# Where r is projected, who adds the diagonal term, and the order of work in the two feed-forward fronts of a hybrid block

## The chip, the core and the metric

The kernel runs on one core of a Trainium2 chip, as one launch. The metric is the device time of that launch in microseconds; lower is better. Engines are named as in the profile: PE is TensorE (PEld its weight loads), DVE is VectorE, ACT is ScalarE, POOL is GpSimd, SP issues most DMAs. Each engine runs its own list of instructions in the order in which the kernel writes them, and the lists meet only at semaphores.

## What is computed

Input x has 2 sequences of 1024 tokens with 128 channels, all float32. Every layer is added to x after a layer norm of its input:

```
x = x + attn_a(layernorm(x))   # 16 heads of 8, decaying state, token shift, group of 32
x = x + ffn(layernorm(x))      # shared SwiGLU + one expert of 32 for each token
x = x + attn_b(layernorm(x))   # 16 heads of 64, blocks of 16, 5 levels of coarse keys
x = x + ffn(layernorm(x))      # the same weights again
```

In attn_a, for one token, `y = inter + intra + diag * v`, with `diag = sum(r * (time_faaaa * k))` over a head. The kernel reads inter and intra together out of one recurrence over the tokens; diag * v is the "diagonal term". In ffn, `scores = sigmoid(max logit)`, the tokens are sorted by expert, and `silu(x g) * (x u)` times d is computed for each group.

## The kernel before, in words

The 2048 tokens are worked in 4 chunks of 512 (STEPS = 4).

**Attention A** (`a_pe`, `a_act`, `a_pool`, `a_dve`, about 0 to 120 us). Each engine has a loop over the chunks c. For one chunk PE projects v, k, r (`project`, L275 and L276: two products of 128x512 each) into the banks WIDE[0..2]; ACT copies them out (`projected`, L500). PE spreads the rows of v over four banks (`spread_rows`, L291), twice per chunk; it waits for the copies of all three of v, k and r. DVE multiplies k by the spread v (`key_value`, L751, 8 per chunk in two fours) and runs the recurrence (`scan`, L757, 8 per chunk). POOL multiplies the states by r (`weigh`, L660), PE sums them per head (`pick`, L299, two halves) into the bank YB. The diagonal term: PE sums r*k per head (`diagonal`, L310), ACT copies it, POOL multiplies it by v (`dv`), and PE adds it to the sums in YB by a product with the identity (`add_diagonal`, L305); ACT copies YB out (`copy_y`, L511). PE turns y (`turn_y`, L317), DVE takes its statistics, ACT normalises, PE turns it back (`turn_back`, L323), ACT copies, PE projects (`project_y`, L334), and DVE adds it to x (`add_output`, L763). Beside this the next chunk is prepared: `turn_x`, `mix_in` (L242), ACT's tanh, `mix_out` (L249), and DVE's `mixed` (L734, after scans 0 and 1 of the chunk before).

**Front of a feed-forward layer** (`f_pe`, `f_act`, `f_dve`, `f_pool`, k = 0 and 1). Per chunk: statistics, `front_norm`, `front_turn` (L999), `front_copy`, `front_logits` (L1009), `route` (DVE, L1028 to L1035: best expert and its one-hot). `count_tokens` counts per expert for each half of the tokens, `first_places` / `second_places` and `row_numbers` turn the counts to row numbers; POOL then scatters each half with 8 indirect DMAs (L1475) to sorted_x. The shared expert runs beside it: `shared_half` (L1157), `gate_shared` (ACT, L1173), `product_shared` (DVE, L1179), `shared_out` (L1166), `add_shared` (L1184). Two places hold products whose result nobody reads: L1203 (k = 0) and `keep_clock` (L1194). Then 24 runs of 128 sorted rows follow (L1253 and on), each group of 32 rows with its expert's weights.

**Attention B** (`b_pe` and its companions, about 200 to 450 us). It begins with 4 unread products (L1709), x's first two chunks normalised by DVE (L1464) with POOL's power (L178), turned, copied by ACT and projected (L1738). Then come 16 units of two heads. `project_out` (L1831) of a unit needs POOL's product of output and reciprocal (L2210, two halves), and DVE adds it to x (`gather_out`, L2060). After the last unit the second front begins: `first_slots`, the sums of chunks 2 and 3, and so on.

## Time and profile before

| | us |
|---|---|
| median of the runs shown | 547.14 (545.95 to 549.12) |
| the profiled execution, its own time | 546.38 |
| its span in the trace | 544.6 |
| mean granted TensorE clock | 0.974 of full |

| engine | busy us | share |
|---|---|---|
| PE | 489.6 | 90% |
| PEld | 300.6 | 55% |
| DVE | 424.8 | 78% |
| ACT | 290.7 | 53% |
| POOL | 251.4 | 46% |

Read it by stages: attention A to about 120 us, first front to 150, first runs to 200, attention B to 450, second front to 485, second runs to the end. A timeline row names an instruction (or a row of like ones), its start, its length, and in brackets how long its engine had stood idle before it and whose result ended that. A share of busy time is a mean over stages; what a wait is worth is read from the stage where it stands.

### The profile page before, as it was taken

What the parts mean: (1) busy time and instruction counts of PE and PEld (TensorE: products, weight loads), DVE (VectorE), ACT (ScalarE), POOL (GpSimd) and SP (SyncE); (2) the same over time, 40 slices, a digit from 0 to 9 for tenths busy, and PEclk for the clock granted to TensorE, in tenths of its full rate; (3) what the DMA queues carried; (4) which work ended last, traced back from release to release, by engine and by line L of the source; (5) the groups of instructions that cost most, each with busy time, mean ns of one, the idle gap of its engine ahead of it and who ended that gap; (6) DMA issues with size and microseconds to landing.
All of it is one profiled execution on the core that took longest, in us unless ns stands there. A gap on an engine that the chain in (4) does not pass through costs nothing.

```text
span 544.6 us, 16679 instructions
## 1 busy us (share of the span) xinstructions
PE 489.6 (90%) x6456; PEld 300.6 (55%) x6456; DVE 424.8 (78%) x979; ACT 290.7 (53%) x624; POOL 251.4 (46%) x294
## 2 busy tenths in 40 slices
PE   6899899778999988999989999999999778989991
PEld 3323333344545445677767777677767666444540
DVE  3498899987557767788898888998978987657762
ACT  3743533446288835566455655456544324448870
POOL 3578766746425461533544433333313535524542
PEclk9999999989999989999999999999999987999996
DMA  6799840001588832000000000000000000268964
GB/s 186 305 427 300 83 49 2 0 0 41 165 234 271 269 104 69 17 22 22 22 17 27 23 14 17 14 22 22 22 22 9 6 4 19 57 189 280 279 205 139
DMA packets 45326, 54.11 MB, mean 99 GB/s; under 512 B 10880, under 2 KB 36416, under 8 KB 44224
## 3 DMA queue, kind: packets, MB, share of 16 engines
q1 hardware_dynamic: 42688, 47.78, 30.3%
q0 software_dynamic: 2560, 5.26, 2.8%
q8 instruction: 52, 0.85, 0.7%
q14 instruction: 26, 0.21, 0.1%
HBM read 43.55 MB, written 9.48 MB: 97 GB/s over the span
## 4 chain that ended last, share of the span: by engine, by line
PE 61%; DVE 22%; issue 5%; POOL 4%; DMA 3%; ACT 3%; SPq 0%; POOLq 0%; DVEq 0%; ACTq 0%
PE psum L1253 9%; PE psum L1738 7%; PE psum L1756 7%; PE psum L1831 5%; PE psum L1272 4%; PE psum L1810 4%; PE psum L1260 3%; DVE arena L757 3%; POOL sorted_x L1475 2%; PE psum L1779 2%; PE psum L275 2%; DVE arena L2040 2%; PE psum L1820 2%; DVE arena L2035 2%; DVE arena L2081 2%
## 5 line engine op out<-in xcount | busy, mean ns | idle before, releaser
L2210 POOL TENSOR_TENSOR arena<-arena 128x512 f32<-128x512 f32 x32 | 40.9, 1299 | 108.4 <-issue 102.2
L1503 POOL DMA_INDIRECT y_tok<-arena,to x48 | 46.5, 969 | 64.9 <-ACT arena L1322 63.7
L1926 ACT ACTIVATE arena<-psum 128x512 f32<-128x512 f32 x64 | 37.9, 597 | 45.2 <-PE psum L1738 42.0
L1738 PE MATMUL psum<-arena 128*128 128x512 f32 x128 | 59.2, 605 | 0.8 <-ACT arena L1909 0.7
L1253 PE MATMUL psum<-experts,arena 128*32 x96 | 50.2, 604 | 1.0 <-ACT arena L1312 1.0
L1253 PE MATMUL psum<-arena 128*32 128x512 f32 x288 | 50.9, 605 | 0.0
L1756 PE MATMUL psum<-arena 128*128 128x128 f32 x384 | 47.5, 278 | 1.5 <-ACT arena L1931 1.5
L1756 PEld LDWEIGHTS psum<-arena 128*128 128x128 f32 x384 | 45.2, 191 | 2.5 <-ACT arena L1931 2.5
L2147 POOL TENSOR_TENSOR arena<-arena 128x256 f32<-128x256 f32 (+4 forms) x75 | 33.9, 451 | 24.9 <-ACT arena L1945 18.3
L660 POOL TENSOR_TENSOR arena<-arena 128x512 f32<-128x512 f32 x32 | 37.1, 1180 | 16.4 <-DVE arena L757 12.0
L1738 PEld LDWEIGHTS psum<-arena 128*128 128x128 f32 x128 | 22.9, 189 | 35.6 <-issue 34.0
L1336 ACT ACTIVATE arena<-experts 128x768 f32 x48 | 40.1, 839 | 1.9 <-issue 1.7
L1399 DVE COPY arena<-psum 128x256 f32<-128x256 f32 x48 | 20.4, 425 | 25.0 <-PE psum L1260 25.0
L1475 POOL DMA_INDIRECT sorted_x<-arena,row x32 | 31.1, 973 | 18.6 <-DVE row L1103 10.1
L757 DVE TENSOR_TENSOR_SCAN arena<-psum,arena 128x512 f32<-128x512 f32 x32 | 39.2, 1267 | 0.1
L1810 PE MATMUL psum<-arena 64*64 64x64 f32 (+2 forms) x1728 | 36.8, 224 | 2.4 <-ACT arena L1941 1.5
L1934 ACT ACTIVATE arena<-psum 128x512 f32<-128x512 f32 x48 | 28.7, 598 | 16.4 <-PE psum L1756 16.4
L1272 PEld LDWEIGHTS psum<-experts,arena 128*32 128x32 f32 x192 | 20.7, 110 | 29.8 <-issue 29.6
L2060 DVE TENSOR_TENSOR x_tok<-x_tok,psum 128x512 f32<-128x512 f32 x30 | 20.6, 687 | 20.8 <-PE psum L1831 20.7
L1810 PEld LDWEIGHTS psum<-arena 64*64 64x64 f32 x1728 | 33.0, 137 | 6.5 <-ACT arena L1941 1.6
L1831 PE MATMUL psum<-arena 128*128 128x128 f32 x256 | 34.0, 286 | 2.7 <-POOL arena L2210 2.7
L2034 DVE TENSOR_REDUCE arena<-psum 128x16 f32<-128x1024 f32 (+1 forms) x32 | 30.4, 950 | 3.4 <-PE psum L1779 2.9
(240 smaller groups left out, 1180.6 us busy)
## 6 DMA issues: line engine op xcount, KB each, us to landing
arena<-in_experts SPq DMA_DIRECT2D x48, 384.0 KB, 4.4
experts<-in_experts SPq DMA_DIRECT2D x8, 1536.0 KB, 17.7
arena<-sorted_x SPq DMA_DIRECT2D x48, 64.5 KB, 3.9
sorted_x<-zeros SPq DMA_DIRECT2D x2, 1536.0 KB, 15.3
arena<-in_w_qkv SPq DMA_DIRECT2D x16, 192.0 KB, 3.1
arena<-y_tok SPq DMA_DIRECT2D x8, 256.0 KB, 3.2
x_tok<-in_x SPq DMA_DIRECT2D x4, 256.0 KB, 4.3
arena<-in_w_out SPq DMA_DIRECT2D x16, 64.0 KB, 1.9
```

The costliest lines, as they stand in the source:

```text
L757: dve.tensor_tensor_scan(a_state[:, m, 1:CHUNK + 1], DECAYS[:, :], a_kv[m % HALF], a_state[:, m, 0:1], ALU.mult, ALU.add).then_inc(s["stat ...
L1253: mm = pe.matmul(bank[2 + s % 2][rows, :], f_gxt[s % 2][:, rows], weights, start=True, stop=True)
L1272: mm = pe.matmul(bank[6 + s % 2][SLOT_ROWS * j:SLOT_ROWS * j + SLOT_ROWS, 0:C], f_sht[s % 2][:, rows], weights, start=(half == 0), stop=(h ...
L1336: act.activation(f_w_act[s % 5], experts[:, bass.ds(expert_at[s], WROW)], ACT.Copy).then_inc(t["w_act"], 1)
L1475: pool.indirect_dma_start(out=sorted_x[k], out_offset=bass.IndirectOffsetOnAxis(ap=f_row[:, i:i + 1], axis=0), in_=row_of(k, i), in_offset ...
L1503: pool.indirect_dma_start(out=y_tok, out_offset=bass.IndirectOffsetOnAxis(ap=f_to[:, s:s + 1], axis=0), in_=f_gy[(s + 4) % 8], in_offset=N ...
L1738: pe.matmul(ring("in", n, j)[:, :], b_w[n % 2][:, which * P:which * P + P], x, start=True, stop=True)\
L1756: mm = pe.matmul(ring("in", n, 5 + i // 4)[:, i % 4 * P:i % 4 * P + P], x, b_w[n % 2][:, 2 * P:3 * P], start=True, stop=True)
L1810: mm = pe.matmul(place(Y[r][out]), b_v[n % 2][rows, i, out], e[rows, head, i - part.start, cols], start=(i == 0), stop=last_place(r, i, cols))
L1831: mm = pe.matmul(ring("out", n, i // 4)[:, i % 4 * C:i % 4 * C + C], b_yn[:, i * P:i * P + P], b_wo[n % 2], start=(n < LAST - 1 or n < LAS ...
L1926: act.activation((b_q, b_k)[which][:, part * CHUNK:part * CHUNK + CHUNK], src, ACT.Copy, scale=(D_B ** -0.5, 1.0)[which]).then_inc(h["drai ...
L2210: pool.tensor_tensor(b_yn[:, part], b_y[:, part], b_rec[:, part], ALU.mult).then_inc(h["normed"], 1)
```

## The change

Attention A. `project(c, 2)`, the projection of r, moves from the end of chunk c - 1 to behind `spread_rows(c, 0)`, and goes to the bank OB instead of WIDE[2]; `spread_rows(c, 0)` now waits for the copies of v and k alone, `mix_in(c)` for that of r. `add_diagonal` on PE and `copy_y` on ACT are gone; `outputs(c)` on DVE adds YB and the diagonal term into a_y, behind scan(c + 1, 1), and for the last chunk behind the first route. `turn_back` and `copy_back` of the earlier chunks go to the start of the chunk after next.

First front (k = 0). The two unread products go; the second product of the shared expert's chunk 0 goes behind `route` of chunk 3.

Start of attention B. The add of chunk 1's expert outputs is done in the last runs, both powers are behind each other on POOL ahead of the last two scatters, two unread products instead of four, and q and k are projected chunk by chunk (`project_half`, `drain_half`).

End of attention B and second front (k = 1). Five short unread products (`fill_wait`) stand around the last unit's coarse scores. The second half of the last unit's output is multiplied by DVE (`normalise_late`) and not by POOL. The shared expert's first pair of products goes ahead of the last `project_out`, three unread products behind. `first_slots` goes behind the last sums, `first_places` behind the last chunk's norm, `shared_out` behind `count_tokens`, and `add_shared(0)` behind `slot_experts`, which is the tail of `second_places`, now its own function. `keep_clock` is left out for k = 1.

```diff
                 pe.wait_ge(s["mixers"], 2)
-                after(pe, s["decay_exp"], c)
+                after(pe, s["rkv"], 3 * c)
...
-                if c > 0:
+                if n == 2:
+                    pe.wait_ge(s["decay_exp"], c + 1)
+                elif c > 0:
                     pe.wait_ge(s["kv"], N_A * (c - 1) + HALF + n + 1)
-                pe.matmul(WIDE[n][:, :], weights, a_x[c % 2][:, 1:CHUNK + 1], start=True, stop=False)
-                pe.matmul(WIDE[n][:, :], weights, a_t[(2, 1, 3)[n]], start=False, stop=True).then_inc(s["proj"], 1)
+                pe.matmul(PROJECTED[n][:, :], weights, a_x[c % 2][:, 1:CHUNK + 1], start=True, stop=False)
+                pe.matmul(PROJECTED[n][:, :], weights, a_t[(2, 1, 3)[n]], start=False, stop=True).then_inc(s["proj"], 1)
 
             def spread_rows(c, q):
                 if q == 0:
                     pe.wait_ge(s["rows"], 1)
-                    pe.wait_ge(s["rkv"], 3 * c + 3)
+                    pe.wait_ge(s["rkv"], 3 * c + 2)
                     pe.wait_ge(s["shifted"], 2 * c + 2)
...
-            def add_diagonal(c):
-                pe.wait_ge(s["dv"], c + 1)
-                pe.matmul(YB[:, :], ident, a_diag, start=False, stop=False).then_inc(s["dvacc"], 1)
 
...
             project(0, 0)
             turn_x(1)
-            project(0, 2)
 
...
                 if now:
                     spread_rows(c, 0)
-                if back and now:
-                    add_diagonal(c - 1)
+                    project(c, 2)
+                if 2 <= c < STEPS:
+                    turn_back(c - 2)
...
                     pe.wait_ge(s["kv"], N_A * c + HALF + 1)
                     front_turn(pe, 0, 0)
                     keep_busy_last(1)
                     pe.wait_ge(loaded_later, LATER_LOADS * 16)
                     front_logits(pe, 0, 0)
-                if next_:
-                    project(c + 1, 2)
-                if back:
+                if c >= STEPS - 1:
                     turn_back(c - 1)
...
                     after(act, s["g"], N_A * (c - 1))
-                act.activation((a_v, a_k, a_r)[n][c % 2], WIDE[n][:, :], ACT.Copy).then_inc(s["rkv"], 1)
+                act.activation((a_v, a_k, a_r)[n][c % 2], PROJECTED[n][:, :], ACT.Copy).then_inc(s["rkv"], 1)
 
             def copy_diagonal(c):
                 act.wait_ge(s["diag_in"], c + 1)
-                after(act, s["dvacc"], c)
+                after(act, s["y"], c)
                 act.activation(a_diag, YB[:, :], ACT.Copy).then_inc(s["diag"], 1)
-
-            def copy_y(c):
-                act.wait_ge(s["picked"], 2 * c + 2)
-                act.wait_ge(s["dvacc"], c + 1)
-                after(act, s["yt"], c)
-                act.activation(a_y, YB[:, :], ACT.Copy).then_inc(s["y"], 1)
 
...
+            heads_and_rows()
             projected(0, 0)
-            heads_and_rows()
             copy_x(1)
-            projected(0, 2)
-            norm_x(2)
             for c in range(STEPS + 1):
                 now, next_, later_, back = c < STEPS, c + 1 < STEPS, c + 2 < STEPS, 1 <= c
                 if now:
                     decay(c)
+                    if c == 0:
+                        norm_x(2)
+                    projected(c, 2)
...
 
+            def outputs(c):
+                dve.wait_ge(s["picked"], 2 * c + 2)
+                dve.wait_ge(s["dv"], c + 1)
+                after(dve, s["yt"], c)
+                dve.tensor_tensor(a_y, YB[:, :], a_diag, ALU.add).then_inc(s["y"], 1)
+
...
                 for m in range(HALF):
                     key_value(c, m)
+                scan(c, 0)
+                scan(c, 1)
+                if back:
+                    outputs(c - 1)
                 if c == STEPS - 1:
                     dve.wait_ge(s["rkv"], 3 * STEPS)
                     row_ids(dve, 0)
-                scan(c, 0)
-                scan(c, 1)
...
             add_output(STEPS - 2)
             route(dve, chain, 0, 0, 1)
+            outputs(STEPS - 1)
...
                 front_logits(pe, k, 2)
-                for _ in range(2):
-                    pe.matmul(rows_bank(k, 3)[:, :], ident, shared_up[:, :], start=True, stop=True)
                 front_turn(pe, k, 3)
                 front_logits(pe, k, 3)
                 count_tokens(pe, k, 1)
                 shared_out(pe, k, 0)
+                shared_half(pe, k, 1, 0, 1)
             else:
                 front_turn(pe, k, 2)
+                front_logits(pe, k, 2)
                 front_turn(pe, k, 3)
-                front_logits(pe, k, 2)
                 front_logits(pe, k, 3)
+                shared_half(pe, k, 1, 0, 1)
+                count_tokens(pe, k, 1)
                 shared_out(pe, k, 0)
-                count_tokens(pe, k, 1)
-            shared_half(pe, k, 1, 0, 1)
             shared_half(pe, k, 1, 1, 2)
-            keep_clock(2)
+            if k == 0:
+                keep_clock(2)
             shared_half(pe, k, 2, 0)
...
             else:
                 gate_shared(act, k, 0, 0)
+                gate_shared(act, k, 0, 1)
                 front_norm(act, k, 2)
-                gate_shared(act, k, 0, 1)
                 front_copy(act, k, 2)
                 front_copy(act, k, 3)
...
                 row_ids(dve, k)
-                first_places(dve, chain, k)
-                row_numbers(dve, chain, half_of(k, 0), 0)
             c = STEPS - 1
...
             if k == 1:
+                first_places(dve, chain, k)
+                row_numbers(dve, chain, half_of(k, 0), 0)
+                route(dve, chain, k, 2, 2)
+                product_shared(dve, k, 0, 1)
+                second_places(dve, chain, k)
+                slot_experts(dve, chain, k)
+                add_shared(dve, k, 0)
                 for n in range(2):
-                    product_shared(dve, k, 0, n)
-                route(dve, chain, k, 2, 2)
+                    product_shared(dve, k, 1, n)
             else:
                 route(dve, chain, k, 2, 1)
+                product_shared(dve, k, 0, 0)
+                route(dve, chain, k, 3, 1)
+                product_shared(dve, k, 0, 1)
+                second_places(dve, chain, k)
+                slot_experts(dve, chain, k)
+                add_shared(dve, k, 0)
                 for n in range(2):
-                    product_shared(dve, k, 0, n)
-                route(dve, chain, k, 3, 1)
-            if k == 1:
-                add_shared(dve, k, 0)
-            second_places(dve, chain, k)
-            if k == 0:
-                add_shared(dve, k, 0)
-            for n in range(2):
-                product_shared(dve, k, 1, n)
+                    product_shared(dve, k, 1, n)
             done(dve, "slot_row", 1)
             chain(dve.tensor_scalar(f_slot_row[0:1, :], bank[7][0:1, 0:SLOTS], float(WROW), None, ALU.mult))
...
                     chain(add_experts(dve, k, 0))
+                    chain(add_experts(dve, k, 1))
...
-                    norm_power(pool, LN_B, b_stats[0][:, 1:2 * CT:2], b_rstd[0])
+                    for c in range(2):
+                        norm_power(pool, c + LN_B, b_stats[c][:, 1:2 * CT:2], b_rstd[c])
 
...
                     if i % 4 == 0:
-                        pe.wait_ge(h["normed"], 2 * n + i // 4 + 1)
+                        if n == LAST and i:
+                            pe.wait_ge(h["normed_late"], 1)
+                        else:
+                            pe.wait_ge(h["normed"], 2 * n + i // 4 + 1)
                         if n < LAST:
...
-            pe.wait_ge(h["x"], 2)
-            for which in range(2):
-                for part in range(2):
-                    project(0, which, part)
+            for r in range(2):
+                pe.wait_ge(h["x"], r + 1)
+                for which in range(2):
+                    project_half(which, r)
             pe.wait_ge(masks, 2)
             scores(0, FINE)
             pe.wait_ge(h["packed"], 1)
...
+                if n == LAST:
+                    pe.wait_ge(h["acc"], 2 * (LAST - 1))
+                    fill_wait(CHUNK + CHUNK // 2)
                 if now:
                     scores(n, ROUGH)
+                if n == LAST:
+                    fill_wait(CHUNK)
                 if new:
                     project_last(n + 1)
...
                 else:
+                    pe.wait_ge(h["y_out"], UNITS)
+                    shared_half(pe, 1, 0, 0)
                     project_out(n - 1)
-                    pe.wait_ge(h["y_out"], UNITS)
-                    for half in range(2):
-                        shared_half(pe, 1, 0, half)
+                    shared_half(pe, 1, 0, 1)
+                    pe.wait_ge(h["z_out"], UNITS)
+                    for _ in range(3):
+                        pe.matmul(bank[7], ident, const[:, 0:CHUNK], start=True, stop=True)
 
         def b_act(act):
...
             def statistics(c):
-                chain(add_experts(dve, 0, c))
+                if c > 1:
+                    chain(add_experts(dve, 0, c))
...
 
+            def normalise_late():
+                part = slice(CHUNK, SEQ)
+                dve.wait_ge(h["y_out"], UNITS)
+                dve.wait_ge(h["o"], 2 * LAST)
+                dve.tensor_tensor(b_yn[:, part], b_y[:, part], b_rec[:, part], ALU.mult).then_inc(h["normed_late"], 1)
+
...
                     front_inverse(dve, chain, 1)
                 if n == UNITS:
-                    first_slots(dve, chain, 1)
+                    normalise_late()
+                    product_shared(dve, 1, 0, 0)
                 if n < LAST:
...
                 pool.wait_ge(h["y_out"], n + 1)
-                for j in range(2):
```

Three places, as the engines' lists have them (L numbers of before and of after differ).

PE, the fourth chunk of attention A, from the first pick of the third, before:

```order
L299 MATMUL psum<-arena 32x512 x4
L275 MATMUL psum<-arena 128x512
L276 MATMUL psum<-arena 128x512
L323 MATMUL psum<-const,arena 128x128 x4
L291 MATMUL psum<-arena 128x512 x4
L305 MATMUL psum<-arena,const 128x512
L299 MATMUL psum<-arena 32x512 x4
L317 MATMUL psum<-const,arena 128x128 x4
L310 MATMUL psum<-arena 128x512
L334 MATMUL psum<-arena 128x128 x4
L291 MATMUL psum<-arena 128x512 x4
```

and after:

```order
L302 MATMUL psum<-arena 32x512 x4
L294 MATMUL psum<-arena 128x512 x4
L278 MATMUL psum<-arena 128x512
L279 MATMUL psum<-arena 128x512
L322 MATMUL psum<-const,arena 128x128 x4
L302 MATMUL psum<-arena 32x512 x4
L316 MATMUL psum<-const,arena 128x128 x4
L309 MATMUL psum<-arena 128x512
L333 MATMUL psum<-arena 128x128 x4
L294 MATMUL psum<-arena 128x512 x4
```

L291 and after it L294 is `spread_rows`, L275/L276 and L278/L279 `project`, L305 `add_diagonal`, L323/L322 `turn_back`, L299/L302 `pick`, L317/L316 `turn_y`, L310/L309 `diagonal`, L334/L333 `project_y`. The spreading no longer stands behind r and `turn_back`; `turn_y`, `diagonal` and `project_y` keep their order.

DVE, the same chunk, before:

```order
L751 TENSOR_TENSOR arena<-arena,psum 128x512 x4
L1077 TENSOR_SCALAR arena<-const,place_col 128x16
L757 SCALAR_TENSOR_TENSOR arena<-psum,arena 128x512 x2
L763 TENSOR_TENSOR x_tok<-x_tok,psum 128x512
L969 BN_STATS arena<-x_tok 128x6 x4
L973 BN_AGGR arena<-arena 128x2 x4
L976 TENSOR_SCALAR arena<-arena 128x4
```

and after:

```order
L739 TENSOR_TENSOR arena<-arena,psum 128x512 x4
L745 SCALAR_TENSOR_TENSOR arena<-psum,arena 128x512 x2
L752 TENSOR_TENSOR arena<-psum,arena 128x512
L1074 TENSOR_SCALAR arena<-const,place_col 128x16
L757 TENSOR_TENSOR x_tok<-x_tok,psum 128x512
L966 BN_STATS arena<-x_tok 128x6 x4
L970 BN_AGGR arena<-arena 128x2 x4
```

Line L752 is `outputs(2)`: it stands ahead of `add_output` (L763, after L757), and its result is what `turn_y` on PE turns.

DVE in the second front, before, from the row numbers of the first half to the scan of `second_places`:

```order
L1103 CAST row<-arena 128x8
L1368 TENSOR_SCALAR arena<-x_tok,arena 128x128 x4
L1179 TENSOR_TENSOR arena<-arena,psum 128x512 x2
L1028 TENSOR_REDUCE arena<-psum 128x8
L1029 TENSOR_TENSOR arena<-psum,arena 128x256
L1030 TENSOR_TENSOR arena<-arena,const 128x256
L1031 TENSOR_REDUCE arena<-arena 128x8
L1035 TENSOR_TENSOR one_hot<-const,arena 128x256
L1184 TENSOR_TENSOR x_tok<-x_tok,psum 128x512
L1126 TENSOR_TENSOR psum<-psum,arena 128x32
```

and after:

```order
L1366 TENSOR_SCALAR arena<-x_tok,arena 128x128 x4
L1116 TENSOR_TENSOR arena<-arena 128x256
L1117 TENSOR_TENSOR arena<-arena 128x256
L1098 TENSOR_TENSOR arena<-arena,one_hot 128x256
L1099 TENSOR_REDUCE arena<-arena 128x8
L1100 CAST row<-arena 128x8
L1025 TENSOR_REDUCE arena<-psum 128x8
L1026 TENSOR_TENSOR arena<-psum,arena 128x256
L1027 TENSOR_TENSOR arena<-arena,const 128x256
L1028 TENSOR_REDUCE arena<-arena 128x8
L1032 TENSOR_TENSOR one_hot<-const,arena 128x256
L1179 TENSOR_TENSOR arena<-arena,psum 128x512
```

The norm of the last chunk (L1368, after L1366) now stands ahead of the row numbers of the first half, and `add_shared` (L1184) no longer stands ahead of `second_places` (L1126; after, L1123 is the next row behind those shown).

## Rows read from the trace of the kernel before

**Rows 1.** Busy us by engine, granted clock, DMA share, GB/s in four windows.

```profile
70.00:95.00 25.00, 22.93 (x102) 9.15 (x95) 23.20 (x54) 8.66 (x16) 17.65 (x16) 1.00 0.18 15
118.00:119.00 1.00, 1.00 (x3) 0.37 (x2) 0.97 (x5) 0.00 (x0) 0.22 (x1) 0.50 0.00 0
300.00:400.00 100.00, 98.49 (x1916) 74.69 (x1919) 87.43 (x166) 56.13 (x115) 37.00 (x57) 1.00 0.07 20
460.00:461.00 1.00, 1.00 (x6) 1.00 (x6) 0.85 (x2) 0.00 (x0) 0.70 (x2) 0.50 0.20 66
```

**Rows 2.** Timeline, attention's first chunk: start, us, engine, line, form, [idle <-releaser].

```profile
21.74 0.60 ACT L500 ACTIVATE arena<-psum 128x512 f32<-128x512 f32 x1 [1.16 <-PE psum L276]
...
24.60 1.14 PE L291 MATMUL psum<-arena 32*128 32x512 f32 x8 [0.73 <-issue]
...
25.89 2.48 DVE L751 TENSOR_TENSOR arena<-arena,psum 128x512 f32<-128x512 f32 x4 [4.61 <-PE psum L291]
...
30.66 1.39 DVE L734 SCALAR_TENSOR_TENSOR arena<-psum,vectors,arena 128x512 f32<-128x512 f32 x2
```

**Rows 3.** Timeline, attention's second chunk.

```profile
44.20 2.48 DVE L751 TENSOR_TENSOR arena<-arena,psum 128x512 f32<-128x512 f32 x4 [0.37 <-PE psum L291]
...
46.53 0.60 ACT L511 ACTIVATE arena<-psum 128x512 f32<-128x512 f32 x1 [0.33 <-PE psum L299]
...
46.60 2.45 DVE L757 TENSOR_TENSOR_SCAN arena<-psum,arena 128x512 f32<-128x512 f32 x2
...
48.22 0.60 PE L317 MATMUL psum<-const,arena 128*128 128x128 f32 x4
...
49.07 1.14 PE L249 MATMUL psum<-arena 32*128 32x512 f32 x8 [0.25 <-ACT arena L465]
...
50.28 1.41 DVE L734 SCALAR_TENSOR_TENSOR arena<-psum,vectors,arena 128x512 f32<-128x512 f32 x2 [1.23 <-PE psum L249]
```

**Rows 4.** Timeline, attention's third and fourth chunks.

```profile
65.17 2.48 DVE L751 TENSOR_TENSOR arena<-arena,psum 128x512 f32<-128x512 f32 x4 [1.17 <-PE psum L291]
...
70.80 1.41 DVE L734 SCALAR_TENSOR_TENSOR arena<-psum,vectors,arena 128x512 f32<-128x512 f32 x2 [0.58 <-PE psum L249]
...
89.14 2.45 DVE L757 TENSOR_TENSOR_SCAN arena<-psum,arena 128x512 f32<-128x512 f32 x2
...
90.55 1.05 PE L334 MATMUL psum<-arena 128*128 128x128 f32 x8
...
91.64 0.69 DVE L763 TENSOR_TENSOR x_tok<-x_tok,psum 128x512 f32<-128x512 f32 x1
```

**Rows 5.** Timeline, the first feed-forward front.

```profile
122.51 1.96 PE L1203 MATMUL psum<-shared_up,const 128*128 128x512 f32 x4
...
126.72 0.29 DVE L1028 TENSOR_REDUCE arena<-psum 128x4 f32<-128x128 f32 x1 [1.09 <-PE psum L1009]
...
135.06 0.96 POOL L1475 DMA_INDIRECT sorted_x<-arena,row  x1 [2.99 <-DVE row L1103]
```

**Rows 6.** Timeline, the start of the second attention.

```profile
199.53 4.84 PE L1709 MATMUL psum<-const 128*128 128x512 f32 x8
...
203.48 1.12 DVE L1464 TENSOR_SCALAR arena<-x_tok,arena 128x128 f32<-128x128 f32 x4 [1.96 <-POOL arena L178]
...
206.00 3.70 PE L1738 MATMUL psum<-arena 128*128 128x512 f32 x8 [0.69 <-ACT arena L1909]
```

**Rows 7.** Timeline, the second attention's end and the second front.

```profile
445.07 2.89 POOL L2210 TENSOR_TENSOR arena<-arena 128x512 f32<-128x512 f32 x2 [2.32 <-DVE arena L2051]
...
448.02 2.07 PE L1831 MATMUL psum<-arena 128*128 128x128 f32 x8 [0.41 <-POOL arena L2210]
...
460.10 0.42 DVE L1028 TENSOR_REDUCE arena<-psum 128x8 f32<-128x256 f32 x1 [2.26 <-PE psum L1009]
...
464.10 0.69 DVE L1184 TENSOR_TENSOR x_tok<-x_tok,psum 128x512 f32<-128x512 f32 x1 [1.67 <-PE psum L1166]
...
470.82 0.96 POOL L1475 DMA_INDIRECT sorted_x<-arena,row  x1 [4.38 <-DVE row L1103]
```

45 lines of the change are left out of this document (30 added, 15 removed).

## Prediction

> **What bounds the kernel now.** I read the windows first, then the timeline of each place that the change touches, engine by engine. In attention A DVE has work almost all the time (23.20 of 25 us) while PE, though 22.93 us busy, waits on it and feeds it; in attention B it is PE (98.49 of 100 us) [rows 1]. So in A each us added to DVE, or to what DVE waits for, is a us of the kernel. In B a shift of the start passes through unchanged. In the two fronts a chain of single steps across four engines sets the time, and there the granted clock matters: in parts of them it is 0.50, which is 1.2 GHz instead of 2.4 [rows 1]. The five unread products of the last unit stand where PE waits for DVE's subtraction; about 0.5 us each (a quarter of the 1.96 us of [rows 5]) lies under that wait, and without that cover they would cost 2.5 us.
>
> **Attention A: four steps, and they lose.**
> Start. DVE stands idle 4.61 us until the first spreading is done. That began at 24.60, although v had been copied out at 21.74 + 0.60 = 22.34 [rows 2]; it waited for the copy of r. Now it can begin at 22.4, 2.2 us sooner. But r (two products, 1.96 us by [rows 5]) now stands between it and the next chunk's preparation. From 22.4: spreading 1.1, r 1.9, turn 0.7, `mix_in` 1.9, tanh 0.7, `mix_out` 1.2, so DVE's `mixed` starts near 30.0 instead of 30.66 [rows 2]. Gain 0.65, not 2.2.
>
> Second chunk. DVE's wait of 0.37 before its products goes [rows 3]. Then comes the new order. Before, from the products (44.20) to `mixed` (50.28) took 6.08 us, 1.23 of it waiting for `mix_out`. `turn_y`, which stands ahead of `mix_out` on PE, could start right after ACT's copy of y at 46.53, so it cost nothing. After, y comes from DVE, behind two scans. The products take 2.40, two scans 2.45, the add 0.65, then `turn_y` 0.60, `mix_out` 1.14, and three hand-overs of some 0.07: 7.4 us [rows 3]. Instead of 6.08 this is 1.3 more. What is queued behind the waiting `turn_y` on PE is all of the next chunk's preparation; DVE waits for that some 1.9 us. With 0.65 and 0.37 gained, and 1.3 lost, A is 0.3 late here; I take 0.2, since rounding went against the change.
>
> Third chunk. The wait of 1.17 goes (PE no longer stands behind r and `turn_back`). From products to `mixed` it was 70.80 - 65.17 = 5.63 and becomes 7.4 [rows 4]: 1.8 more. A is 0.2 - 1.2 + 1.8 = 0.8 late, and about 0.5 after the boundary that follows, where another wait of the kind in [rows 3] goes.
>
> Fourth chunk. There is no `mixed`, but `add_output(1)` stands behind the scans. Before, it came at 91.64 with no wait, as its product on PE (90.55, 1.05 us) was done [rows 4]. After, that product stands behind `turn_y(2)`, which waits for DVE's add. The scans end at 89.14 + 2.45 = 91.6, the add at 92.2, `turn_y` 0.65, `diagonal` 1.0, `project_y` 1.0, with hand-overs: 95.1 instead of 91.64, so 3.4; less the small row-number step that now lies in the gap, 3.1. A is 3.6 late.
>
> Last chunk's y. ACT's copy becomes DVE's add (0.65), and DVE also waits some 0.3 for the last pick, less 0.2 that it waited before for `turn_y`: 0.8. **A together: +4.4 us.** The bounds: 0, if only the four adds count (2.6) and the removed waits (0.65 + 0.37 + 1.17 + 0.37 = 2.6) pay for them; and +6, if PE's new pause of 3 us in the fourth chunk lets the clock fall, so that 2.6 us of work ahead of `add_output` takes half as long again or more.
>
> One price can be looked at by itself. Here an add out of a bank takes DVE 0.69 us [rows 4], and a plain copy out of one takes ACT 0.60 [rows 3]. The Trainium skill ("VectorE: DVE Perf Modes", Specifications) says that ScalarE sits closer to PSUM than VectorE, which speaks against this move; the two rows agree in sign. By it alone the move would cost 4 times 0.09 = 0.4 us; the waits above are ten times that.
>
> **First front (k = 0).** Two unread products go (1.96 us on PE [rows 5]). The last chunk's turn comes 1.6 sooner, but ACT is still in its two gates, so its copy gains 1.0; `route` then ends 0.9 sooner, where DVE idled 1.09 at 126.72. The product moved behind it takes 0.65 and covers DVE's wait for the counts. The row numbers, for which POOL idled 2.99 [rows 5], gain 0.8. The chain of the shared expert runs beside it: it gains 0.5, and PE finishes it as the first rows arrive. So -0.5. Against it stands the clock. The products removed were PE's work in a stretch where it otherwise has two turns and some small logits, and before, after a pause of the same kind, the clock was 0.50 at 118 [rows 1]. Some 3 us at half rate on PE's chain cost up to 1.5, so +1.0. I take the middle, **0**; bounds -0.9 (both chains gain what the row numbers do) and +2.
> The Trainium skill ("TensorE: Matmul & The Clock Gate", What's actually happening) says that the default state is the throttled one and that activity releases it. The fall at 118 agrees. By that rule the front ends 1.0 later, by the row of the removed products alone 0.5 sooner.
>
> **Start of attention B.** Before: four unread products from 199.53, 4.84 us, and DVE's second normalisation at 203.48 after a wait of 1.96 for POOL's power, which stood behind two scatters; projection from 206.00, 3.70 us [rows 6]. After: both powers follow each other, so the second normalisation is about 2.4 sooner minus 0.4 for the add of chunk 1, now done in the last runs and delaying their last step. PE, with two unread products, turns x at 202.6. The first chunk is projected once its own copy is there, about 203.9, and the four products end near 207.7 instead of 209.7. The rest of the first unit follows PE: **-1.8**. DVE's coarse queries no longer start half-way; it gains only 1.2 there, but has slack in the next unit. The last two scatters come 1.1 later, and their read-back is needed 9 us on, so that costs nothing. Bounds -2.3 and -0.5 (fewer fillers leave the clock at half rate into the projection: 3.7 us of it).
>
> **End of B and second front.** POOL's two halves from 445.07 took 2.89, and PE's last four pairs began at 448.02 at the low clock and took 2.07 [rows 7]. After, DVE does one half in about 0.65 beside POOL's other, the fillers keep the clock, and PE ends that step near 447.8 instead of 449.9: 2.1 sooner, and so are the sums and the last norm. Then the logits at the full clock: `route` starts at 457.4 instead of 460.10. Then the order: before, `second_places` stood behind `add_shared` at 464.10, which waited 1.67 for a slow `shared_out`, and ended at 464.7 [rows 7]; after, it follows `route` (2.3) and one product (0.65): 460.4. That is 4.3 sooner. POOL's second eight scatters started at 470.82 after 4.38 idle [rows 7]; now POOL itself is late, since the first half's row numbers stand behind the last norm, and starts them at 466.7: 4.1. The shared expert's chain pays 0.65 for `add_shared` ahead of its products and gains 3.7, the least of these. **-3.7.** Bounds -4.6 and -1.5 (if the clock stays at 0.50 there, as at 460 [rows 1]).
>
> **Sum.** 4.4 + 0 - 1.8 - 3.7 = -1.1. Against the profiled execution's own 546.4 (span 544.6 and 1.8 around it) that is 545.3; that execution lay 0.8 under the median of 547.14, so on the scale of the median **546.0**.
>
> **The rivals.**
> Attention A costs nothing. PE's preparation might lie so far ahead that DVE meets no new wait, and the adds are paid by the waits removed. For it: four waits of 0.37 to 4.61 do go [rows 2 to 4]. Against it: `turn_y` is ahead of `mix_out` in PE's list, and DVE waited there already. Then 0 + 0 - 1.8 - 3.7 = -5.5: 541.6.
>
> The clock falls where PE now pauses. The place is the fourth chunk of A, then the first front and the start of B. Its price is 1.4 + 1.0 + 1.0, and if the second front stays at 0.50 as before, another 2.2: 4.4 + 1.4 + 1.0 - 0.8 - 1.5 = +4.5, 551.6; with the first and the last only half, near 549.5. It decides as soon as the lost high clock costs over 3.8 us together, 1.1 plus the 2.7 of the bound below. For it: 118 and 460 [rows 1]. Against it: in A the clock was 1.00 all through 70 to 95 [rows 1], and fillers were put into the last unit.
>
> The second front gains nothing, as the transfer of sorted rows is the end anyway: against it stands POOL's idle 4.38 [rows 7]; it would give 549.7. I give it little.
>
> **How the numbers follow.** What a measurement of this kernel can tell from no change is 0.5%, 2.7 us. Forecast 0.52; A costs nothing 0.25; the clock falls 0.18; no gain in the second front 0.05. Half the width of the forecast's own terms is some 2.5 us, so a little of it reaches under 544.4. Faster 0.30, same 0.49, slower 0.21. The range 541.5 to 549.8 takes in the first rival and the near half of the second. The forecast's own is 543.5 to 548.5.
>
> **What would show it.** In the profile after: DVE waits 1.5 to 2 us before `mixed` in the second and third chunk, and 2.5 to 3 before `add_output` in the fourth; the loop of A ends 3 to 4 us later than before. The waits before the first products of chunks 2 to 4 are gone. The second projection's start is 2 us nearer to the end of the first runs. Counted from the last unit, the second runs begin 3.7 sooner, and the clock is 1.00 there. The prediction is wrong if `mixed` follows the add without a wait, or if the clock is 0.50 in stretches other than before.

## The result, and the profile after

Twenty runs of each kernel: the changed kernel took 550.05 us (median; 547.00 to 554.62), the kernel before 546.88 us (545.40 to 550.56), a ratio of 1.0066 with a 95% interval of 1.0045 to 1.0087. It is 0.66% slower, a small change but clear of its interval. The forecast was 546.0 with a range to 549.8, so the median lies just outside it, on the other side of no change.

The profiled execution happened to be the slowest of the twenty (554.62 us, span 552.7). A second profile of the same kernel is of an execution of 547.41 us (span 545.5). The table shows how late each place is against the kernel before, in both. Reading the two beside each other tells what the order of work costs each time, and what only some executions pay.

| place (us in the profile before) | first profile | second profile |
|---|---|---|
| DVE's first product of A (25.89) | -2.02 | -2.24 |
| `mixed` in the second chunk (50.28) | +0.60 | +0.38 |
| `mixed` in the third chunk (70.80) | +1.13 | +0.91 |
| `add_output(1)` (91.64) | +5.81 | +5.08 |
| last `add_output` of A (117.57) | +8.31 | +6.05 |
| first result scattered in the first runs (157.60) | +9.76 | +5.66 |
| first projection of B (206.00) | +7.23 | +3.98 |
| sums of chunk 2 behind B (449.71) | +5.00 | +1.94 |
| first of POOL's second eight scatters (470.82) | +4.73 | +1.13 |
| first result scattered in the second runs (492.63) | +8.23 | +1.02 |
| span (544.6) | +8.1 | +0.9 |

DVE's timeline of attention A in the changed kernel, first profile (start, us, engine, line, operation, count, idle time before and what ended it). L739 are the products of k, L745 the scans, L752 the new add, L722 `mixed`, L1074 the small row-number step, L757 `add_output`:

```profile
43.60 2.48 DVE L739 TENSOR_TENSOR arena<-arena,psum 128x512 f32<-128x512 f32 x4
46.00 2.45 DVE L745 TENSOR_TENSOR_SCAN arena<-psum,arena 128x512 f32<-128x512 f32 x2
48.37 0.66 DVE L752 TENSOR_TENSOR arena<-psum,arena 128x512 f32<-128x512 f32 x1
50.88 1.41 DVE L722 SCALAR_TENSOR_TENSOR arena<-psum,vectors,arena 128x512 f32<-128x512 f32 x2 [1.85 <-PE psum L250]
...
71.93 1.41 DVE L722 SCALAR_TENSOR_TENSOR arena<-psum,vectors,arena 128x512 f32<-128x512 f32 x2 [1.85 <-PE psum L250]
...
92.16 0.66 DVE L752 TENSOR_TENSOR arena<-psum,arena 128x512 f32<-128x512 f32 x1
92.74 0.75 DVE L1074 TENSOR_SCALAR arena<-const,place_col 128x16 f32<-128x16 f32 x1
97.45 0.69 DVE L757 TENSOR_TENSOR x_tok<-x_tok,psum 128x512 f32<-128x512 f32 x1 [3.96 <-PE psum L333]
```

The reader sees the three waits that the prediction named. Products to `mixed` is 50.88 - 43.60 = 7.28 us, where it was 6.08 [rows 3]. The waits ahead of the products [rows 3 and 4] are gone. The last wait is the large one, 3.96 us against none at 91.64 [rows 4]; 2.5 to 3 was predicted (second profile 3.44). The loop of A ends 5.9 and 6.0 us later than before, where 3 to 4 was said. PE's own rows there, `turn_y`, `diagonal` and `project_y`, say why:

```profile
88.54 1.06 PE L302 MATMUL psum<-arena 128*32 128x512 f32 x8 [1.40 <-POOL arena L648]
92.88 1.12 PE L316 MATMUL psum<-const,arena 128*128 128x128 f32 x4 [3.27 <-DVE arena L752]
93.79 1.92 PE L309 MATMUL psum<-arena 128*128 128x512 f32 x2
95.50 1.92 PE L333 MATMUL psum<-arena 128*128 128x128 f32 x8
```

PE stood idle 3.27 us for DVE's add and then ran at the lower clock: 1.92 us each for what took 1.02 and 1.05 in the kernel before (PE at 89.69 and 90.55). Windows of the kernel before, and then of the first and the second profile of the changed kernel (busy us of PE, PEld, DVE, ACT, POOL, granted clock, DMA share, GB/s):

```profile
88.00:98.00 10.00, 8.83 (x44) 4.02 (x40) 9.81 (x22) 2.85 (x6) 6.68 (x7) 1.00 0.01 2
...
120.00:140.00 20.00, 16.94 (x84) 10.47 (x83) 15.28 (x46) 10.58 (x19) 12.84 (x13) 1.00 0.12 38
```

```profile
88.00:98.00 10.00, 6.19 (x26) 3.88 (x30) 6.04 (x9) 0.60 (x2) 5.00 (x5) 0.66 0.00 1
...
120.00:140.00 20.00, 13.98 (x61) 10.29 (x61) 15.81 (x51) 12.60 (x26) 10.99 (x11) 0.71 0.08 24
```

```profile
88.00:98.00 10.00, 6.40 (x31) 3.57 (x32) 6.52 (x11) 0.60 (x1) 4.78 (x5) 0.83 0.00 1
...
120.00:140.00 20.00, 14.31 (x65) 10.20 (x66) 17.81 (x60) 12.60 (x26) 11.92 (x12) 0.83 0.09 28
```

The low clock now also stands in the fourth chunk of attention A and from 120 to 140 us, where the kernel before had 1.00, and there is more of it in the first profile than in the second. The prediction had named this as a sign that it is wrong (a clock of 0.50 "in stretches other than before"). Over all runs, the mean granted clock had a median of 0.973 in the kernel before (127 runs) and 0.965 in the changed one (32 runs). The three runs of the changed kernel at 0.973 took 547.00, 547.41 and 547.83 us; fourteen of the kernel before at 0.973 had a median of 546.5. So about 1 us of the loss is there at the same mean clock, as the second profile has it (+0.9), and the rest, 2 to 3 us, goes with the lower clock. This is a comparison of executions; it doesn't say which pause costs what.

### The profile page after: what moved, and what is told of

It reads as the page before. It is cut to its first block, busy times and chain, and to the rows that moved or that the text cites. A ratio compares the mean times of both kernels' runs of the same rounds, so it can differ in the third digit from the quotient of the medians.

```text
span 552.7 us, 16670 instructions
## 1 busy us (share of the span) xinstructions
PE 491.6 (89%) x6452; PEld 301.3 (55%) x6452; DVE 427.3 (77%) x984; ACT 288.7 (52%) x620; POOL 250.7 (45%) x293
## 4 chain that ended last, share of the span: by engine, by line
PE 59%; DVE 23%; issue 6%; DMA 4%; ACT 4%; POOL 3%; SPq 0%; DVEq 0%; POOLq 0%; ACTq 0%
PE psum L1253 8%; PE psum L1772 7%; PE psum L1746 7%; PE psum L1850 5%; DVE arena L745 5%; PE psum L1157 4%; PE psum L1826 4%; PE psum L1272 3%; PE psum L1260 3%; DVE arena L739 3%; PE psum L1795 2%; PE psum L1166 2%; PE psum L1836 2%; DVE arena L2121 2%; DVE arena L2118 2%
## 5 line engine op out<-in xcount | busy, mean ns | idle before, releaser
L2251 POOL TENSOR_TENSOR arena<-arena 128x512 f32<-128x512 f32 x31 | 39.2, 1287 | 107.1 <-issue 102.1
L1953 ACT ACTIVATE arena<-psum 128x512 f32<-128x512 f32 x60 | 35.5, 597 | 43.2 <-PE psum L1746 40.0
L1746 PE MATMUL psum<-arena 128*128 128x512 f32 x120 | 55.5, 605 | 0.0
L1772 PEld LDWEIGHTS psum<-arena 128*128 128x128 f32 x384 | 45.2, 191 | 2.5 <-ACT arena L1958 2.5
L648 POOL TENSOR_TENSOR arena<-arena 128x512 f32<-128x512 f32 x32 | 37.1, 1180 | 15.5 <-DVE arena L745 10.4
L1746 PEld LDWEIGHTS psum<-arena 128*128 128x128 f32 x120 | 21.5, 189 | 33.0 <-issue 32.4
L745 DVE TENSOR_TENSOR_SCAN arena<-psum,arena 128x512 f32<-128x512 f32 x32 | 39.2, 1265 | 0.0
L1961 ACT ACTIVATE arena<-psum 128x512 f32<-128x512 f32 x48 | 28.7, 598 | 16.4 <-PE psum L1772 16.4
L1157 PE MATMUL psum<-arena,shared_up 128*128 128x512 f32 x64 | 34.1, 670 | 0.0
```

Source lines behind the costliest of these rows:

```text
L648: pool.tensor_tensor(a_g[m % HALF], a_r[c % 2], a_state[:, m, 0:CHUNK], ALU.mult).then_inc(s["g"], 1)
L745: dve.tensor_tensor_scan(a_state[:, m, 1:CHUNK + 1], DECAYS[:, :], a_kv[m % HALF], a_state[:, m, 0:1], ALU.mult, ALU.add).then_inc(s["stat ...
L1157: pe.matmul(bank[at][:, :], shared_up[:, part * P:part * P + P], turned_rows(k, c), start=True, stop=True).then_inc(t["shared"], 1)
L1746: pe.matmul(ring("in", n, j)[:, :], b_w[n % 2][:, which * P:which * P + P], x, start=True, stop=True)\
L1772: mm = pe.matmul(ring("in", n, 5 + i // 4)[:, i % 4 * P:i % 4 * P + P], x, b_w[n % 2][:, 2 * P:3 * P], start=True, stop=True)
L2251: pool.tensor_tensor(b_yn[:, part], b_y[:, part], b_rec[:, part], ALU.mult).then_inc(h["normed"], 1)
```

## The experiments

Every ratio is to the kernel before, run beside it on the same chip; the brackets are 95% intervals; 0.1% is 0.55 us. The runs of this section are spread over five chips. The three kernels that were measured more than once came out 0.04 to 0.22% apart, so a difference of two ratios under some 0.3% is weak. Of attention A first.

**The changed kernel once more** (no edit).

> The changed kernel itself, once more, beside the runs of the kernel before. Its profiled execution was the slowest of its twenty runs (554.62 us, mean granted clock 0.962; the fastest 547.00 at 0.973). Theory C (the stretches at the low clock fall at different places from one execution to the next, the order of work costs the same each time): the median is again near 550, the wait of DVE before mixed in the second and third chunk is again 1.85 us, and a profile of a faster execution has the granted clock nearer to 1.00 in one or more of 90 to 98, 112 to 118, 122 to 130 and 135 to 143 us. Rival (the low clock is fixed by the program): the granted clock per 20 us is the same as in the first profile, 0.83 at 80 to 100 and 0.71 at 120 to 140.

Measured: 551.47 us, 1.0082 [1.0052, 1.0112]. DVE's waits of 1.85 us came out alike to the hundredth, the granted clock did not (0.83 where 0.66 was). The low clock is not fixed by the program, and the median is near 550 again, as expected.

**The add moved ahead of the scans** (`y_before_scans`).

```
+                if back:
+                    outputs(c - 1)
                 scan(c, 0)
                 scan(c, 1)
-                if back:
-                    outputs(c - 1)
```

> The changed kernel with one move: DVE adds the diagonal term of the last chunk before the first two scans of a chunk, not behind them. Theory W (DVE waits for mix_out because turn_y stands ahead of it on PE and y comes 5 us after the chunk's first product): the waits of 1.85 us before mixed in the second and third chunk and of 3.96 us before add_output(1) fall under 0.3 each, loop of attention A ends (its add_output(2)) near 105 us instead of 111.74, and the median is 544 to 545.5. Rival (the pick of the last rows is no earlier ready, so that DVE waits before its add instead): the idle time moves to the line of the add, 1 us or more in each chunk, and the median stays at 548 or above.

Measured: 543.87 us, 0.9935 [0.9905, 0.9964]. Waits 0.57, 1.23 and 0:

```profile
49.43 1.41 DVE L722 SCALAR_TENSOR_TENSOR arena<-psum,vectors,arena 128x512 f32<-128x512 f32 x2 [0.57 <-PE psum L250]
...
87.81 0.68 DVE L752 TENSOR_TENSOR arena<-psum,arena 128x512 f32<-128x512 f32 x1
88.41 2.45 DVE L745 TENSOR_TENSOR_SCAN arena<-psum,arena 128x512 f32<-128x512 f32 x2
90.78 0.29 DVE L1074 TENSOR_SCALAR arena<-const,place_col 128x16 f32<-128x16 f32 x1
91.00 0.69 DVE L757 TENSOR_TENSOR x_tok<-x_tok,psum 128x512 f32<-128x512 f32 x1
```

The same add on the same engine, two scans earlier, is worth 1.4% (7.6 us against the mean of the changed kernel's two ratios, 1.0074). The first two waits did not fall under 0.3 as expected, because PE's sum of the last rows, which stands ahead of `mix_in`, waits there for POOL; but what DVE's add held up is gone. The loop ended at 105.96, and the median is a little under the 544 to 545.5 expected. PE's row of that wait, in the second chunk:

```profile
44.55 1.06 PE L302 MATMUL psum<-arena 128*32 128x512 f32 x8 [1.40 <-POOL arena L648]
```

**PE's pause filled** (`fill_fourth`): in the fourth chunk, ahead of `turn_y(2)`,

```
+                    for _ in range(3):
+                        pe.matmul(OB[:, :], ident, wrkvo, start=True, stop=True)
```

> The changed kernel with three unread products (512 columns each, about 2.9 us) on PE in its pause of 3.27 us ahead of turn_y(2) in the fourth chunk. They write the bank that project_y overwrites. Theory C (the pause lets the clock fall, and turn_y, diagonal and project_y at half rate make 2 of the 3.96 us before add_output(1)): granted clock 1.00 from 80 to 100 us, that wait 2.0 to 2.4 us, loop end 1.5 to 2 us earlier, median 548 to 549. Rival (the wait for y is all of it): the wait stays above 3.5 us, median within 0.5 us of the changed kernel's.

Measured: 550.23 us, 1.0068 [1.0043, 1.0092]. The granted clock from 88 to 98 us is 1.00, `turn_y`, `diagonal` and `project_y` run as in the kernel before, and the wait is half:

```profile
88.00:98.00 10.00, 8.79 (x40) 4.10 (x41) 8.07 (x19) 0.77 (x2) 5.16 (x5) 1.00 0.00 1
```
```profile
93.04 0.66 PE L316 MATMUL psum<-const,arena 128*128 128x128 f32 x4 [0.51 <-DVE arena L756]
93.53 1.02 PE L309 MATMUL psum<-arena 128*128 128x512 f32 x2
94.40 1.05 PE L333 MATMUL psum<-arena 128*128 128x128 f32 x8
...
95.48 0.69 DVE L761 TENSOR_TENSOR x_tok<-x_tok,psum 128x512 f32<-128x512 f32 x1 [1.83 <-PE psum L333]
```

So of the 3.96 us 2.1 were the clock, and 1.8 the wait for y itself. The low clock behind this pause was no accident of one execution: all four profiles in which PE stood idle 3.27 or 3.28 us here (the two of the changed kernel, `A_part_alone` and `after_fill0`, both below) have it, and their granted clock from 88 to 98 us is 0.66 to 0.83. With the pause filled, `add_output(1)` is 3.84 us late and the last `add_output` 4.81 (122.38), close to the 3.6 and 4.4 of the prediction. In the profile the loop ended 1.1 us earlier (110.65), but the median did not move, and the expected 548 to 549 was missed. Why is not shown. The mean granted clock of the twelve runs had a median of 0.965, as in the changed kernel, so the low clock stood elsewhere in them; from 120 to 140 us it was 0.83 here, as in the second profile.

**y on PE and ACT again** (`y_on_act`, run twice), everything else as changed.

```
 # PE, behind project(c, 2) and, for the last chunk, behind pick(c, 0)
+                if back and now:
+                    add_diagonal(c - 1)
 # ACT, behind copy_x(c + 2)
+                if back:
+                    copy_y(c - 1)
 # DVE
-                if back:
-                    outputs(c - 1)
...
-            outputs(STEPS - 1)
```

> The changed kernel with one part undone: PE adds the diagonal term to the bank and ACT copies y out, as before; r behind the spreading, both fronts and attention B stay as changed. Theory W: the whole loss of attention A is in this part; with it undone the loop of A ends near 104 us (before 105.88, less 0.6 at the start and the gone waits of 1.17 and 0.37), and the median is 542.5 to 544.5, below the kernel before. Rival F (the fronts and the start of B lose): loop end near 104 all the same, but a median at 547 or above.

> y_on_act once more, with more runs: the ratio to the kernel before was 0.9922 with only six runs. If the gain is the mechanism's and not that chip's: ratio 0.990 to 0.995, and the range of its runs under 4 us. Rival (its narrow range of 542.4 to 544.2 was luck, since every kernel of this family has runs 5 us above its fastest): ratio 0.995 to 1.0, range 5 us or more.

Measured: 542.82 us, 0.9922 [0.9894, 0.9950], and 543.36 us, 0.9944 [0.9925, 0.9963], as expected. The last `add_output` came at 116.50, 1.07 us sooner than in the kernel before. Undoing this one part gives 1.4% and turns a loss into a gain.

The profiles show a second price of taking the addition off PE. In the third chunk PE waits for POOL's product ahead of `pick` and then for ACT ahead of `mix_in`. With y on DVE these waits are 1.52 and 0.50 us; with y on PE and ACT, where `add_diagonal` stands ahead of `pick`, they are 0.95 and 0.50; the kernel before waits 1.14 us for ACT at 63.21 and then works through to 69 us. Of the ten profiles of kernels with y on DVE, three have `mix_in` at the low clock (`A_part_alone`, `early_fill0`, `early_bstart_old`); of the nine with y on PE and ACT behind the moved r, none. Three of ten against none of nine is no proof, but it fits that the runs of the first group are, with one exception, the wider ones.

**Attention A's part alone**, on the kernel before: the diff's pieces in `a_pe`, `a_act` and `a_dve` and nothing else (`A_part_alone`), and the same with y as in `y_on_act` (`A_part_y_on_act`). Against the kernel before, the core of the second is

```
 # PE
                     spread_rows(c, 0)
+                    project(c, 2)
+                if 2 <= c < STEPS:
+                    turn_back(c - 2)
...
-                if next_:
-                    project(c + 1, 2)
-                if back:
+                if c >= STEPS - 1:
                     turn_back(c - 1)
```

> The kernel before with the change's part in attention A alone (r behind the spreading, DVE's adds behind the scans, the later turn_back); both fronts and attention B as before. The prediction's term was 4.4 us; the second profile of the changed kernel shows attention A's last add_output 6.05 us later than before. Theory W (a wait in A is a wait of the kernel): that add_output 6 us later than before, and a median of 552.5 to 554.5. Rival (half of it is covered by the first front's other chains): median at or under 550.

> As A_part_alone, but with y summed on PE and copied by ACT as before: what is left of attention A's part is r behind the spreading and the later turn_back. Theory W: the first products 2.2 us earlier, the last add_output 1.1 us earlier, median 545.3 to 546.3. Rival (r behind the spreading makes PE wait in the later chunks, so that the clock falls there as in the changed kernel): median at or above 547.5, with a wider spread than the kernel before.

Measured: 553.88 us, 1.0114 [1.0076, 1.0152], its last `add_output` 8.04 us late; and 545.82 us, 0.9986 [0.9967, 1.0005]. Both medians are as theory W expected: a wait in A is a wait of the kernel. The profiled execution of the first was one that had the low clock in the third chunk too, so it is later than the 6 us expected. The four adds on DVE cost 1.3% (7.0 us); the projection of r behind the spreading gives 0.8 us, or nothing within its interval (its last `add_output` is 0.54 us sooner, 1.1 was expected).

Then the parts behind A. On `y_before_scans`, each part undone alone. The cores of the four edits, `fill0`, `bstart_old`, `bend_old` (its last unit; it has the lines of `front1_old` too) and `front1_old`:

```
 # fill0: PE, first front
+                for _ in range(2):
+                    pe.matmul(rows_bank(k, 3)[:, :], ident, shared_up[:, :], start=True, stop=True)
                 front_turn(pe, k, 3)
 # bstart_old: PE; with it POOL's power, the add of chunk 1 and ACT's copies
-            keep_busy(2)
+            keep_busy(4)
...
-                    project_half(which, r)
+                    project(0, which, part)
 # bend_old: PE, DVE, POOL
-                    fill_wait(CHUNK + CHUNK // 2)
...
-                    normalise_late()
-                    product_shared(dve, 1, 0, 0)
+                    first_slots(dve, chain, 1)
...
-                for j in range(2 if n < LAST else 1):
+                for j in range(2):
 # front1_old: DVE; PE's and ACT's order goes with it
+                first_places(dve, chain, k)
+                row_numbers(dve, chain, half_of(k, 0), 0)
...
                 route(dve, chain, k, 2, 2)
+                add_shared(dve, k, 0)
                 second_places(dve, chain, k)
                 slot_experts(dve, chain, k)
-                add_shared(dve, k, 0)
```

> The kernel y_before_scans (its one profile: 544.08 us, median 543.87, runs from 541.53 to 548.87) with the two unread products put back into the first front, ahead of front_turn(3). Theory C (their absence lets the clock fall in the first front, in some executions more than in others; granted 0.74 at 120 to 130 and 0.92 at 130 to 140 us in that profile): the granted clock from 120 to 140 us is 1.00 as in the kernel before, the slow half of its runs goes, median 542 to 543.3. Rival (they only cost PE 1 to 2 us in the chain of the shared expert and the clock falls elsewhere all the same): median 544 to 545.5, the spread as wide as before.

> y_before_scans with the start of attention B as before: four unread products, POOL's second power behind the two last scatters, chunk 1's experts added in B, projection of both chunks together. The prediction's term: the first projection's end 1.8 us later against the runs' start, median 545.2 to 546. Rival (the first unit waits for something else, so that the earlier projection is given back): median within 0.5 us of 543.9.

> y_before_scans with the last unit of attention B and the second front as before (POOL does both halves of the last normalisation, no unread products in the last unit, gathers and row numbers in the old order). The prediction's term is 3.7 us, the two profiles of the changed kernel show 3.0: median 546.5 to 547.5. Rival (the unread products of the last unit only move the low clock into the front, so that the gain is 1 us or less): median under 545.

> y_before_scans with the second front's order alone as before (row numbers of the first half ahead of the last norm, add_shared(0) ahead of second_places, all turns ahead of the logits, two unread products), the last unit as changed. Theory S (the prediction's: the order brings POOL's second eight scatters forward): they start 1 to 1.5 us later than in y_before_scans counted from the last norm's sums, median 544.8 to 545.6. Rival P (PE's shared expert is the later chain, and the order changes nothing on it; the gain of the second front is the last unit's alone): median within 0.5 us of 543.9.

Measured 0.9964 [0.9939, 0.9989], 1.0014 [0.9993, 1.0035], 1.0012 [0.9987, 1.0036] and 1.0017 [0.9996, 1.0039], that is 1.6, 4.3, 4.2 and 4.5 us over the 0.9935 of their base. The medians of the last three (547.92, 548.10, 547.09) are 0.6 to 1.9 us over the highest that their theories had, and `early_fill0` at 545.55 ended where its rival had it, not theory C. The second and the third come to 8.5 us for attention B and the second front, where the two profiles of the changed kernel show a gain of 1.5 and 4.6 between the first scattered result of the first runs and that of the second. In the profiles of this series that stretch is 332.8 us in the base, 335.0 with `bstart_old`, 332.9 with `bend_old` and 332.7 with `front1_old`: only the start of B is seen there, with 2.2 us. The base is a poor one: it was measured once, on another chip than the four, and its own runs go from 541.53 to 548.87. If its 0.9935 is some 2 us too low, all four differences are too large by that. One pair of executions shows where such runs part. In the third chunk of A, PE's rows of `pick` and `mix_in` in `y_before_scans` and then in `early_bstart_old`, whose instructions are the same up to here:

```profile
64.54 1.06 PE L302 MATMUL psum<-arena 128*32 128x512 f32 x8 [1.52 <-POOL arena L648]
66.11 1.10 PE L243 MATMUL psum<-arena 128*128 128x512 f32 x2 [0.50 <-ACT arena L495]
67.04 1.02 PE L244 MATMUL psum<-arena 128*128 128x512 f32 x2
```
```profile
64.52 1.07 PE L302 MATMUL psum<-arena 128*32 128x512 f32 x8 [1.51 <-POOL arena L648]
66.08 1.79 PE L243 MATMUL psum<-arena 128*128 128x512 f32 x2 [0.50 <-ACT arena L495]
67.67 1.92 PE L244 MATMUL psum<-arena 128*128 128x512 f32 x2
```

The starts agree to 0.03 us; then one execution has the low clock and the other not. In both PE had just stood idle 1.5 and 0.5 us. The Trainium skill ("TensorE: Matmul & The Clock Gate", What's actually happening) says that the chip's watch on the engine's activity runs freely and is not reset when a kernel starts. That could explain this; no run here shows it by itself.

`act_fill0` is `y_on_act` with the edit `fill0`; its runs are close together, so it became the base.

> y_on_act with the two unread products put back into the first front. Theory F (they cost PE about 1 us in the shared expert's chain and hold no clock, as early_fill0 suggests): from attention A's last add_output to the first scatter of results 1 us longer than in y_on_act (41.5 us), median 0.5 to 1.2 us above it. Theory C (they hold the clock): that stretch shorter than in y_on_act, median at or below it.

> act_fill0 once more, as the base of the next three: ratio to the kernel before 0.9911 with six runs. Theory C (its stretches at the low clock are the fewest of all kernels here, mean granted clock 0.974 to 0.982): ratio 0.989 to 0.993, median 541 to 542.5. Rival (the two products cost as much as they save, as early_fill0 against y_before_scans had it): ratio 0.994 to 0.997, as y_on_act.

Measured: 541.69 us, 0.9911 [0.9884, 0.9938], and 542.27 us, 0.9907 [0.9875, 0.9938]: the fastest of all, 0.9% under the kernel before. Against `y_on_act` (mean 0.9933) the two products gain 0.24%, 1.3 us, though the intervals overlap; what theory F expected, a loss, did not come. The profiles agree with theory C: from the last `add_output` of A to the first scattered result it is 41.52 and 42.02 us in `y_on_act`, and 39.82 and 38.69 with the two products. On it, the same edits, and the last unit's part of `bend_old` without the order (`act_unit_old`):

> act_fill0 with the start of attention B as before. The prediction's term is 1.8 us; early_bstart_old had 0.8% on a base whose own runs are wide. Theory P (the term is right): 1.5 to 2.2 us above act_fill0_again, ratio 0.994 to 0.995. Rival (the start is worth 4 us, as early_bstart_old had it): ratio 0.998 or more.

> act_fill0 with the last unit of attention B and the second front as before. The prediction's term is 3.7 us (2.1 before the last norm, 1.6 behind it); profiles show 2.1 and 0.4 to 0.9. Theory D (the first of the two is right, the second a third of it): 2.5 to 3 us above act_fill0_again, ratio 0.996. Rival: 3.5 us or more, ratio 0.998.

> act_fill0 with the second front's order alone as before. Theory D (behind the last norm the new order gains a third of the 1.6 us predicted, because POOL's first row numbers now wait behind the norm and its sixteen scatters end as late as before): 0.4 to 1 us above act_fill0_again. Rival (early_front1_old: 0.8%, 4 us, since first row numbers ahead of the last norm hold up DVE there and the clock falls in the wait): 3 us or more.

> act_fill0 with the last unit of attention B alone as before (POOL does both halves, no unread products there), the second front's order as changed. Theory D (the last unit brings the last norm's sums 2.1 us forward and all of that reaches the end): 2 us above act_fill0 (542.3, ratio 0.9907), ratio 0.994 to 0.995, the sums 2 us later counted from B's first projection. Rival (additive reading of the last call, 1.7 us for both undone and 2.3 for the order alone: the last unit is worth nothing): ratio 0.989 to 0.992.

Measured: 0.9958 [0.9936, 0.9981], 0.9943 [0.9913, 0.9974], 0.9944 [0.9922, 0.9966] and 0.9970 [0.9952, 0.9989]. Over the base's 0.9909 the start of B is worth 2.7 us, the last unit with the second front 1.9, the order alone undone costs 1.9, the last unit alone 3.3 (this one on another chip than the base). None of the four fell where its favoured theory had it: 1.5 to 2.2, 2.5 to 3, 0.4 to 1 and 2 us were expected. The order and the last unit cost 5.2 us when undone one by one and 1.9 together. The profiles of both series, one execution each, show why, in us:

| end of B and second front | first projection of B to the sums of chunk 2 | sums to POOL's second eight | sums to first result |
|---|---|---|---|
| both old: before, `early_bend_old`, `act_bend_old` | 243.71, 243.48, 245.11 | 21.11, 21.12, 21.32 | 42.92, 42.32, 42.56 |
| order old: `early_front1_old`, `act_front1_old` | 241.51, 241.51 | 23.67, 23.67 | 45.62, 45.51 |
| last unit old: `act_unit_old` | 245.44 | 21.85 | 43.73 |
| both new: `y_before_scans`, `act_fill0` twice, `act_bstart_old` | 241.82 to 242.00 | 20.33 to 20.86 | 42.88 to 43.29 |

The new last unit brings the sums forward by some 2 us; behind it the old order loses 2.5 us, and the new order wins that back and no more. With the old order, PE waits for the last chunk's norm at 452.92, and all of its logits run at the low clock (`act_front1_old`, then the base, where the first half of them does not):

```profile
452.92 1.12 PE L1009 MATMUL psum<-const,arena 128*128 128x128 f32 x4 [3.30 <-DVE arena L1382]
453.83 3.46 PE L1019 MATMUL psum<-gate_w,arena 128*128 128x32 f32 x16
```
```profile
450.92 1.08 PE L1019 MATMUL psum<-gate_w,arena 128*128 128x32 f32 x8 [0.69 <-ACT arena L1014]
451.83 0.63 PE L1009 MATMUL psum<-const,arena 128*128 128x128 f32 x4
453.15 1.92 PE L1019 MATMUL psum<-gate_w,arena 128*128 128x32 f32 x8 [0.69 <-ACT arena L1014]
```

Last, the edit `fill0` on the changed kernel itself.

> The changed kernel itself with the two unread products put back into the first front. Theory C (they save 1.4 us there by the clock, as act_fill0 against y_on_act): ratio to the kernel before 1.003 to 1.006. Rival (on this kernel, where PE waits in attention A already let the clock fall, they save nothing, as early_fill0 against y_before_scans): ratio 1.0075 to 1.010, runs over 550 us in at least half.

Measured: 551.37 us, 1.0068 [1.0046, 1.0090], between what the two theories had and no better than without them (1.0066 and 1.0082). So they gave 1.3 us on one base, nothing here, and cost 1.6 us on `y_before_scans`. Whether the first front wants them stays open within -1.3 to +1.6 us.

## Why the prediction was wrong

| part | predicted | by the runs |
|---|---|---|
| attention A | +4.4 | +6.2 (4.2 to 8.3) |
| first front (the products gone) | 0 | -1.6 to +1.3, open |
| start of B | -1.8 | -2.7 |
| end of B, second front | -3.7 | -1.9 |
| sum | -1.1 | 0.0 to +2.9 (kernel: +3.6) |

The whole change but the adds on DVE measured 0.9933, -3.7 us; the parts found for it come to -0.8 + 1.3 - 2.7 - 1.9 = -4.1. The adds alone cost 7.7 us in the changed kernel (0.9933 against 1.0074) and 7.0 on the kernel before. So the adds behind the scans are more than the whole loss, and the rest of the change gains. Against the prediction no single term carries the miss: the 4.4 of attention A lies at the low end of the interval of its measured 6.2, and each of the other rows is known to 1 or 2 us only.

**Attention A, the step that failed.** The mechanism was right: `turn_y` waits for DVE's add, and the waits before `mixed` are 1.85 us where 1.9 was said. The third chunk's lateness came out at 0.9 to 1.1 us (0.8 said). The term that was mis-sized is the fourth chunk's: 95.1 was said for `add_output(1)`, 96.72 and 97.45 were measured. The prediction took `turn_y`, `diagonal` and `project_y` at 0.65 + 1.0 + 1.0 us; after the pause they ran 1.12 + 1.92 + 1.92 (second profile 1.12 + 1.92 + 1.41), 2.3 and 1.8 us more. `fill_fourth`, where they ran at the full clock, has `add_output(1)` 3.84 us late where 3.6 was said: the clock is what was missing. The prediction had this as a bound ("if PE's new pause of 3 us in the fourth chunk lets the clock fall") and as a rival at 0.18, and set against it that the clock was 1.00 all through 70 to 95 before. That was no argument: the longest wait of PE there was 1.06 us, ahead of `project` at 76.67. The same step also left out that the clock would fall in the chunks behind. In the first profile PE's head sums of the last chunk took 1.89 us instead of 1.06, and A lost another 2.5 us between `add_output(1)` and its last one; in the second, 1.0. The prediction had 0.8 for this stretch.

**First front.** Middle of two opposing terms, 0. The chain is 40.03 us long before (last `add_output` to first scattered result), 41.48 and 39.64 after. In the other kernels it is 39.6 to 42.0 without the products and 38.7 to 42.9 with them, so executions differ by more than the term; that both effects are real is likely and not shown.

**Start of B.** -1.8 said, 2.7 by the runs. First result to first projection was 48.40 us, and 45.87 and 46.72 after. Right in mechanism; the size holds within what the intervals allow.

**End of B.** First projection to the last sums: 243.71 before, 241.48 and 241.67 after: -2.2 and -2.0, where -2.1 was predicted.

**Second front.** 1.6 us more were expected behind these sums; by the table above there are none (42.0 to 43.3 us to the first result with both parts new, the first profile aside, and 42.3 to 42.9 with both old). The second step that failed is "POOL ... starts them at 466.7", 4.1 sooner. Counted from the sums of chunk 2, POOL's first scatter moved from 6.8 to 9.7 us, and its second eight from 21.1 only to 20.8 and 20.3 (by the prediction 19.1, 466.7 less 447.6). The prediction knew that the row numbers of the first half now wait behind the last norm; it priced that too low. In the second profile the first eight scatters, from 9.7 us on, take 10.6, and the next can only follow them. POOL's rows of the second profile, the first scatter, the eighth and the first of the second eight, against 470.82 in [rows 7]:

```profile
461.36 1.09 POOL L1478 DMA_INDIRECT sorted_x<-arena,row  x1 [4.63 <-DVE row L1100]
...
470.69 0.95 POOL L1478 DMA_INDIRECT sorted_x<-arena,row  x1 [0.30 <-DVE row L1100]
471.95 0.96 POOL L1478 DMA_INDIRECT sorted_x<-arena,row  x1 [0.30 <-issue]
```

POOL no longer stands idle between the halves (4.38 before), it stands idle ahead of the first: the wait moved, and the last scatter came 29.7 and 29.2 us behind the sums, where it was 30.0. In the first profile, the first scattered result came 46.15 us behind the sums, some 4 more than in the second. The shared expert's product ran at the low clock in both (3.76 and 3.61 us, where four such rows take 1.88 to 1.99 at the full one), so it doesn't tell them apart. In the first, PE got the sorted rows 6.7 us after the start of the last scatter and not 4.8, and its first runs were at the low clock. Why the rows came later is open. The first profile, then the second:

```profile
491.10 0.33 PE L1198 MATMUL psum<-const,arena 128*128 128x128 f32 x1 [1.42 <-DMA arena<-sorted_x]
...
494.17 1.08 PE L1253 MATMUL psum<-arena 128*32 128x512 f32 x3
```
```profile
485.63 0.33 PE L1198 MATMUL psum<-const,arena 128*128 128x128 f32 x1 [0.25 <-DMA arena<-sorted_x]
...
488.31 0.63 PE L1253 MATMUL psum<-arena 128*32 128x512 f32 x3
```

**The rivals.** "Attention A costs nothing" fell. "The clock falls where PE now pauses" is nearest to what happened: its place in the fourth chunk was right, and its 549.5 to 551.6 holds the measured 550.05. That the number fits so well is in part luck: it had 1.4 us for the fourth chunk where 1.8 to 2.3 were measured, and 1.0 for the start of B where nothing was lost. "The second front gains nothing" took away all 3.7; the 2.1 ahead of the sums came, the 1.6 behind them did not. The forecast gave these two chances of their own and took them for exclusive; they came in part together, and a quarter of the chance went to a rival on the other side. The parts by the runs still leave 0.7 to 3.6 us of the measured 3.6 without an owner; the intervals of the ratios are nearly as wide as that.

## What to carry to other kernels

Before moving an operation to a busier engine, ask what stands behind its consumer in the other engine's list: here the four adds took 2.7 us together and cost the kernel 7.0 to 7.7 behind two scans; two scans earlier they cost next to nothing (0.9935 against 0.9933 without them). Ask also what the operation did where it stood: the product that went from PE had covered a part of a pause. Where an edit opens a pause on PE of a few us, price the matmuls behind it at the low clock and not at the rows of before, even where the clock never fell. If a kernel's own runs spread over 7 us, compare parts on a version that spreads less, and run that version on the same chip.

## What the runs showed of the hardware that was not expected

The granted clock differs between executions whose instructions are the same up to there and start within 0.03 us of each other: products of 1.10 and 1.79 us at 66 us in the rows above. Behind the longer pause of the fourth chunk, 3.27 or 3.28 us, it fell in four executions of four; behind the 1.52 and 0.50 us of the third chunk in three of ten; behind 0.95 and 0.50 us there in none of nine. With the clock goes the time: the 32 runs of the changed kernel lie between 547.0 us at a mean clock of 0.973 and 556.2 us at 0.959, while the twelve of `act_fill0`, at a median of 0.979, lie between 540.6 and 544.0.
